# Fused cross-attention and mixture-of-experts kernel: a third buffer for weight quarters, 128-row reads of the K and Q stacks, filler products in the first slot, and a product between the two score groups

## The chip, the cores and the metric

One Trainium2 chip, one core of it. The time is device microseconds (us) from launch to end of one execution; the profiled execution also has a span, from its first to its last instruction.

## The reference

Two residual blocks over eight batches of 256 x 512. The first is a cross-attention whose positions are the 512 columns, with 16 heads of 16 channels. The second is a mixture of 12 experts, of which each of the 2048 rows uses two.

```python
q = Wq @ layernorm(x) + bq ; k = Wk @ ctx + bk ; v = Wv @ ctx + bv     # per batch, 256x512
scores = einsum('bhkt,bhks->bhts', q, k) * SCALE                       # 16 heads, 512 x 512
out = einsum('bhts,bhks->bhkt', softmax(scores), v)
x = x + tanh(g_xattn) * (Wo @ out + bo)
t = layernorm(x)                                                       # 2048 tokens of 512
probs = softmax(t @ gate_w.T); top_w, top_i = top_k(probs, 2)          # renormalised
for e in range(12):
    h = silu(t @ w1[e].T) * (t @ w3[e].T)                              # 320 wide
    y = y + h @ w2[e].T * cw[:, e:e + 1]
x = x + tanh(g_ffn) * y
```

## The kernel before

**Stages.** Each engine runs its own program, in order; semaphores join them. Attention runs first, then a short routing stage, then 43 expert tiles. Attention is a software pipeline over ten slots (`slots`, L355): slot t projects batch t ("a"), computes scores, exponentials and values of batch t-1 ("b_"), finishes batch t-2 ("c"), and prepares the input of batch t+1 ("p"). Slot 0 only projects batch 0; slots 2 to 6 do all four things; slot 7 has no "p", slot 8 has only "b_" and "c", slot 9 only "c".

**A slot.** It has 16 steps v. In a step TensorE (PE) issues the scores of step v+1 in two groups (L1190, one group for each of the PSUM tensors S0 and S1), then at most one extra product of the table `EXTRA` (steps 0 to 3: k0, k1, q0, q1; 4, 5, 6, 10: v0 to v3; 7 to 9: the output projection o0, o1; 12, 13: transposes t0, t1; 14: the gate's logits), then the values of step v (L1229). ScalarE (ACT) makes two exponentials a step (L716), 128x1024 each. VectorE (DVE) takes every product out of PSUM: k and q by L901, with a cast to a high part (L908), v by L913, the values' sums by L964 after every fourth step, o by L930, the transposes by L933. It also normalises x (L847, cast L852), casts the next context (L832, step 11), and multiplies by the inverse sums (L888, cast L890, step 5). GpSimd (POOL) subtracts each high part from its float32 source to make the low part (L575, L596).

**Quarters.** The experts' float32 weights are split into a high and a low float16 part during attention, in 48 quarters of 512 KB. ACT loads a quarter into one of two buffers `wf` (L691), DVE splits it (L812, L814; `split_quarter`) into one of two buffers `wp`, and ACT stores it (L697; `store_quarter`) and then issues the load of the quarter two later. `quarters` (L334) places the splits at steps: 2, 4, 7, 11, 12, 13 in a steady slot, 4, 7, 11, 13 in slot 1, eight in slot 8. The store of a split at step v stands in ACT's program behind the second exponential of step min(v+2, 15), so ACT waits there until the split is done.

**K and Q.** Their high and low parts are written to DRAM (L491, three parts of 256 KB each) and read back as stacks of 48 rows at partitions 0 and 64 (L498: two DMAs of 384 KB each for K and for Q), because a score product contracts 3 parts x 16 channels. SyncE (SP) issues these. In a slot its queue holds, in order: next context and x (L432, L436), the row of sums (L465, tile `zl`), eight moves of sums (L474) with the write of their inverses between them (L470), eight reads of the inverses (L481), K and Q writes, then, after all six writes have landed, all four reads, then the output (L505) and the normed tokens (L510). DVE makes the inverses (L972) at step 1, ahead of k1's copy.

Of the kernel before, what the change touches and what calls it, by code (L numbers as in the profile page):

```python
# [14 lines left out]
P = 128  # L15
# [34 lines left out]
class Signals:  # L50


    def __init__(self, sem):
# [13 lines left out]
        self.qkst = sem("qkst")  # L67
# [17 lines left out]
        self.raw = sem("raw")  # L85
        self.top = sem("top")
        self.turned = sem("turned")
        self.shift = sem("shift")
        self.shst = sem("shst")
        self.shld = sem("shld")  # L90


def flamingo_kernel(nc, x, ctx_in, g_xattn, g_ffn, WqT, bq, WkT, bk, WvT, bv, WoT, bo, gateT, wall, out):
# [28 lines left out]
    EB = 4  # L122
    HB = 2 * (FT - 1) + 1
# [5 lines left out]
    q_dram = nc.dram_tensor("q_parts", [P // DK, PARTS, DK, CT * T], F16).ap()  # L129
    k_dram = nc.dram_tensor("k_parts", [P // DK, PARTS, DK, CT * T], F16).ap()  # L130
# [10 lines left out]
    with top:  # L141
# [25 lines left out]
        wf = [sb(f"wf{i}", [P, WQ], F32) for i in range(2)]  # L167
# [17 lines left out]
        ctx_sb = [sb(f"ctx{i}", [P, CT, T], F32, att) for i in range(2)]  # L185
# [101 lines left out]
        fast = Signals(lambda name: sem("f_" + name))  # L287
        slow = Signals(lambda name: sem("g_" + name))
# [3 lines left out]
        s_rows = sem("s_rows")  # L292
# [36 lines left out]
        KQ_WRITES, KQ_READS = 16 * 2 * PARTS, 16 * 4  # L329
# [4 lines left out]
        def quarters(t):  # L334

            if t.i is None and t.add in (0, B + 1):
                return []
            if t.i is None and t.add == 1:
                steps, parts = (4, 7, 11, 13), [(At(None, 0, 0), c) for c in range(4)]
            elif t.i is None and t.add == B:  # L340
                steps = (0, 2, 4, 6, 8, 10, 12, 13)
                parts = [(At(None, 0, e), c) for e in (NE - 2, NE - 1) for c in range(4)]
            else:
                steps = (2, 4, 7, 11, 12, 13)
                if t.i is None:
                    e = [At(None, 0, 3 * ((t.add - 2) // 2) + n) for n in (1, 2, 3)]
                else:
                    e = [At(t.i, 3, n) for n in (1, 2, 3)]
                if t.add % 2 == 0:
                    parts = [(e[0], c) for c in range(4)] + [(e[1], c) for c in range(2)]  # L350
                else:
                    parts = [(e[1], c) for c in range(2, 4)] + [(e[2], c) for c in range(4)]
            return [(v, e, c) for v, (e, c) in zip(steps, parts)]
# [21 lines left out]
        s_wf = [sem(f"s_wf{i}") for i in range(2)]  # L375
# [49 lines left out]
        def _(sp):  # L425
            def attention(sp, g, guard):
# [4 lines left out]
                def load_ctx(b, par):  # L431
                    sp.dma_start(ctx_sb[par][:, :, :],  # L432
                                 c_v[bass.ds(b.value(), 1)].rearrange("b p m t -> p (b m) t")).then_inc(g.cc, 16)
# [5 lines left out]
                def slot(sp, t, par, a, b_, c, p):  # L439
# [12 lines left out]
                    if p:  # L452
# [4 lines left out]
                        wait(sp, g.cl, nxt, 1, -1)  # L457
                        load_ctx(nxt, 1 - par)
                        load_x(nxt)
                    if c:  # L460
# [5 lines left out]
                        for half in range(2):  # L466
                            for j in range(GH):
                                if (half, j) == (1, 0):
# [8 lines left out]
                        for half in range(2):  # L477
                            for j in range(GH):
# [3 lines left out]
                    if a:  # L482

                        wait(sp, g.qk, t, KQ_READS, 0, s_bog)
                        for stack, parts, dram, hi, lo, order in ((K, ks, k_dram, g.kh, g.kl, (0, 0, 1)),
                                                                  (Q, qs, q_dram, g.qh, g.ql, (0, 1, 0))):
                            wait(sp, hi, t, 1, 1)
                            for r in sorted(range(PARTS), key=lambda r: order[r]):
                                if order[r] == 1:
                                    wait(sp, lo, t, 1, 1)  # L490
                                sp.dma_start(dram[:, r], parts[:, order[r]].rearrange("p m t -> p (m t)"))\  # L491
                                    .then_inc(g.qkst, 16)

                        wait(sp, g.qkst, t, KQ_WRITES, KQ_WRITES, s_bog)
                        wait(sp, g.full, t, 2 * VS, -2 * VS)
                        for stack, dram in ((K, k_dram), (Q, q_dram)):
                            for s in range(2):
                                sp.dma_start(stack[par][64 * s:64 * s + PARTS * DK, :, :]  # L498
                                             .rearrange("p (g m) t -> p g (m t)", m=CT),
                                             dram.rearrange("(g s) r c n -> s (r c) g n", s=2)[s]).then_inc(g.qk, 16)  # L500
# [11 lines left out]
                if guard:  # L512
                    sp.wait_ge(s_rows, 4)
                load_ctx(At(None, 0, 0), 0)
# [31 lines left out]
        def _(pool):  # L546
# [9 lines left out]
            pool.wait_ge(s_pool_c, 5)  # L556
            def constants():

                pool.tensor_copy(ident16[:, :], ident[:, :]).then_inc(s_vone, 1)
# [11 lines left out]
            def attention(pool, g, guard):  # L571
# [11 lines left out]
                def slot(pool, t, par, a, b_, c, p):  # L583
                    nxt, bc = t.before(-1), t.before(2)
                    if a:
# [11 lines left out]
                    if p:  # L597
                        lo_part(nxt, cs, ctx_sb[1 - par], g.ch, g.cl)

                first = At(None, 0, 0)  # L600
# [850 lines left out]
```

## Time and profile before

| | |
|---|---|
| median of 3 runs | 824.47 us (821.6 to 824.72) |
| profiled execution, its own time | 824.88 us |
| its span | 823.1 us |
| PE busy | 646.0 us (78%) |
| DVE busy | 415.7 us (50%) |
| ACT busy | 316.8 us (38%) |
| POOL busy | 243.8 us (30%) |
| mean granted PE clock | 0.888 |

A share of busy time is a mean over stages. Attention fills the span to about 517 us; the expert tiles run from about 551 us on with PE busy throughout. "Granted clock" is TensorE's clock as the throttle let it through: 1.00 is 2.4 GHz, 0.50 is 1.2 GHz.

### The profile page before, as it was taken

Reading aid. Unit: us, or ns where it says so; the run is one execution under the profiler, and the core shown is the slowest. Engines: PE = TensorE matmul, PEld = TensorE weight load, DVE = VectorE, ACT = ScalarE, POOL = GpSimd, SP = SyncE. Lnnn points to the kernel's source line nnn. Section 1 sums busy time; section 2 is a strip of 40 time slices with the busy share of each in tenths; the row PEclk is TensorE's granted clock in tenths of the full one; section 3 lists DMA queues with packets and bytes.
Section 4 is the critical chain, followed back from the end, with each engine's and each line's share of the span. In section 5 each row is a group of like instructions: output and inputs, shape, how many; then the busy total and the mean of one; then the engine's idle time right before and its main releaser. Section 6 shows DMA issues by size and latency. Waiting matters only on the chain.

```text
span 823.1 us, 13989 instructions
## 1 busy us (share of the span) xinstructions
PE 646.0 (78%) x4217; PEld 282.8 (34%) x4218; DVE 415.7 (50%) x757; ACT 316.8 (38%) x391; POOL 243.8 (30%) x186
## 2 busy tenths in 40 slices
PE   4478897887885977978878654259999999999993
PEld 1112122212221222221221121236666666666661
DVE  5526476566584683774654843563333333333330
ACT  0047655554663554654646510002222222222221
POOL 5223123132240340331210202043344443354422
PEclk9999999889897997997987955559999999999997
DMA  6548669569579587695797636543677787754432
GB/s 205 129 104 204 209 212 293 146 191 310 156 217 293 146 227 262 192 251 159 238 251 211 203 106 230 174 156 63 174 188 195 213 242 201 204 105 92 85 51 39
DMA packets 66405, 150.82 MB, mean 183 GB/s; under 512 B 9973, under 2 KB 15606, under 8 KB 64822
## 3 DMA queue, kind: packets, MB, share of 16 engines
q1 hardware_dynamic: 34576, 72.37, 31.5%
q10 hardware_dynamic: 22150, 55.35, 20.3%
q0 software_dynamic: 9632, 22.55, 14.1%
q8 instruction: 21, 0.34, 0.2%
q14 instruction: 26, 0.21, 0.1%
HBM read 87.85 MB, written 57.93 MB: 177 GB/s over the span
## 4 chain that ended last, share of the span: by engine, by line
PE 50%; DVE 16%; DMA 15%; issue 7%; ACTq 3%; ACT 2%; SPq 2%; POOL 2%; PEldq 1%; POOLq 0%; DVEq 0%
PE S L1365 15%; PE O L1386 8%; DMA wf<-wall 8%; PE O L1229 7%; PE MA L1264 7%; DVE wp L814 4%; PE S L1190 4%; DVE wp L812 4%; DMA out<-yo,slot_out 3%; ACT prob L716 2%; PE S L1352 2%; PE MA L1246 2%; PE MC L1264 2%; ACTq L697 1%; ACTq L691 1%
## 5 line engine op out<-in xcount | busy, mean ns | idle before, releaser
L716 ACT ACTIVATE prob<-S 128x1024 f32<-128x1024 f32 x256 | 244.9, 1025 | 223.5 <-PE S L1190 121.3
L1229 PE MATMUL O<-prob,V 128*32 128x512 f32 x1024 | 154.5, 680 | 0.0
L1365 PE MATMUL S<-W,xT 128*128 x1032 | 150.1, 303 | 1.2 <-issue 1.2
L1190 PE MATMUL S<-Q,K 48*128 48x512 f16 x512 | 93.8, 421 | 69.3 <-ACT prob L716 60.1
L1365 PEld LDWEIGHTS S<-W,xT 128*128 128x128 f16 x1032 | 100.4, 99 | 38.9 <-issue 1.4
L648 POOL DMA_INDIRECT out<-yo,slot_out x43 | 68.2, 1587 | 118.3 <-ACT yo L761 65.4
L1190 PEld LDWEIGHTS S<-Q,K 48*128 48x128 f16 x512 | 19.7, 95 | 209.5 <-ACT prob L716 176.5
L1386 PE MATMUL O<-W,hT 128*128 (+1 forms) x344 | 90.3, 381 | 0.9 <-DVE hT L1161 0.9
L1149 DVE SCALAR_TENSOR_TENSOR hh<-S,act 128x320 f32<-128x320 f32 x43 | 21.1, 492 | 126.9 <-PE S L1365 126.9
L814 DVE SCALAR_TENSOR_TENSOR wp<-wf,wp 128x1024 f16<-128x1024 f32 x48 | 71.4, 1488 | 1.7
L812 DVE TENSOR_SCALAR wp<-wf 128x1024 f16<-128x1024 f32 x48 | 47.0, 979 | 41.9 <-DMA wf<-wall 41.9
L575 POOL TENSOR_TENSOR ks<-kf,ks 128x1024 f16<-128x1024 f32 x8 | 17.0, 2131 | 151.6 <-DVE ks L908 151.6
L624 POOL DMA_INDIRECT xg<-tokens_normed,slot_tok x43 | 42.4, 987 | 46.8 <-PE S L1352 34.6
L761 ACT ACTIVATE yo<-O,slot_w 128x512 f32<-128x512 f32 x43 | 29.5, 687 | 60.5 <-PE O L1386 56.3
L755 ACT ACTIVATE hs<-hh 128x320 f16<-128x320 f32 x43 | 20.2, 470 | 77.8 <-DVE hh L1149 77.8
L748 ACT ACTIVATE act<-S 128x320 f32<-128x320 f32 x43 | 18.8, 437 | 79.9 <-PE S L1365 70.3
L1386 PEld LDWEIGHTS O<-W,hT 128*128 128x128 f16 (+1 forms) x344 | 31.6, 97 | 49.3 <-issue 29.0
L575 POOL TENSOR_TENSOR os<-kf,os 128x1024 f16<-128x1024 f32 x8 | 17.4, 2178 | 89.7 <-DVE os L890 89.7
L1246 PE MATMUL MA<-w4s,cs 128*128 128x256 f16 x192 | 30.1, 300 | 16.0 <-DVE V L913 11.6
L1161 DVE COPY hT<-S 128x640 f16<-128x640 f16 x43 | 21.1, 492 | 41.0 <-PE S L1376 39.1
L1264 PE MATMUL MA<-cs,w4s 128*128 128x512 f16 x96 | 34.8, 519 | 6.9 <-DVE w4s L781 4.1
L901 DVE TENSOR_SCALAR kf<-MA,cols 128x512 f32<-128x512 f32 x16 | 12.0, 751 | 54.3 <-PE MA L1264 54.3
(145 smaller groups left out, 651.5 us busy)
## 6 DMA issues: line engine op xcount, KB each, us to landing
wf<-wall ACTq DMA_DIRECT2D x48, 512.0 KB, 7.6
weight_parts<-wp ACTq DMA_DIRECT2D x48, 512.0 KB, 6.1
W<-weight_parts SPq DMA_DIRECT2D x10, 2048.0 KB, 10.0
k_parts<-ks SPq DMA_DIRECT2D x24, 256.0 KB
q_parts<-qs SPq DMA_DIRECT2D x24, 256.0 KB
K<-k_parts SPq DMA_DIRECT2D x16, 384.0 KB, 7.3
Q<-q_parts SPq DMA_DIRECT2D x16, 384.0 KB, 10.6
ctx<-ctx_in SPq DMA_DIRECT2D x8, 512.0 KB, 10.0
```

Of the source, the lines that this page charges most:

```text
L575: pool.tensor_tensor(parts[:, 1], f[:, :, :], parts[:, 0], ALU.subtract).then_inc(lo, 1)
L624: pool.indirect_dma_start(out=xg[j % TR][:, :], out_offset=None, in_=xn_dram[:, :], in_offset=bass.IndirectOffsetOnAxis(ap=slot_tok[:, j:j ...
L648: pool.indirect_dma_start(out=out[:, :], out_offset=bass.IndirectOffsetOnAxis(ap=slot_out[:, j:j + 1], axis=0), in_=yo[j % TR][:, :], in_o ...
L716: act.activation(prob[:, u % RING, :], S[u % 2][:, :], ACT.Exp, scale=SCALE).then_inc(g.exp, 1)
L812: dve.tensor_scalar(wp[c % 2][:, 0], wf[c % 2][:, :], WS, None, ALU.mult).then_inc(s_whi, 1)
L814: dve.scalar_tensor_tensor(out=wp[c % 2][:, 1], in0=wf[c % 2][:, :], scalar=WS, in1=wp[c % 2][:, 0], op0=ALU.mult, op1=ALU.subtract).then_ ...
L1190: last = pe.matmul(S[u % 2][:, s * T:(s + 1) * T], K[par][r0:r0 + rows_, 2 * g4 + n, st * P:(st + 1) * P], Q[par][r0:r0 + rows_, 2 * g4 + ...
L1229: last = pe.matmul(O[g4 % 2][2 * DK * j:2 * DK * (j + 1), :], V[par][:, st, head(g4, j), :], prob[:, u % RING, (j % 2) * T:(j % 2 + 1) * T ...
L1246: last = pe.matmul(MA[:, i * C:(i + 1) * C], cs[:, xp, k, m * P:(m + 1) * P], w4s[:, wp_, 2, k, :], start=(n == 0 and k == 0), stop=(n == ...
L1264: last = pe.matmul(bank[:, :], w4s[:, wp_, w, k, m * P:(m + 1) * P], src[:, xp, k, :], start=(n == 0), stop=(n == 3 * CT - 1))
L1365: last = pe.matmul(ps, xT[par][:, xp * TT + k, :], W[:, bass.ds(off + (w * WCOL + (2 * k + n) * F), F)], start=(k == 0 and (xp, w) == (0, 0)),
L1386: last = pe.matmul(y_ps[:, :], hT[par][0:rows_, block, :], W[0:rows_, bass.ds(off + (w * WCOL + W2 + k * T), T)], start=(n == 0), stop=(n ...
```

## The change

- Three buffers `wf` in place of two (`WFS = 3`); a store is followed by the load of the quarter three later. The room comes from the context: one buffer in place of two, and the next context's load waits for the low part of the present one.
- The splits of a steady slot are at steps 0, 2, 5, 8, 10, 13; slot 1 has 4, 7, 10, 13; slot 8 is as before.
- The DRAM copies of K and Q get a fourth part, written once at the start (for K with 64, for Q with 0), so that a stack is read as one DMA of 128 rows (1 MB).
- SP issues K's writes, Q's two high writes, then K's read when K's writes have landed, then Q's low write, then Q's read when Q's writes have landed. The semaphore of the writes is split in two.
- The order of the moves of sums and of the reads of inverses is changed; their number is not.
- Slot 0: the low parts of the context, x, K and Q are made by DVE; POOL fills its constants in that time; PE runs filler products (128x128 float32 into an unused part of PSUM): 8 before and 8 after the first product, and the number in `BUSY` behind each projection.
- In a step PE issues the first score group, the extra product, the second score group, the values.

```diff
-            return [(v, e, c) for v, (e, c) in zip(steps, parts)]
+                steps = (0, 2, 5, 8, 10, 13)
+                first = At(t.i, 12, 4 + 6 * (t.add - 2)) if t.i is not None else At(None, 0, 4 + 6 * (t.add - 2))
+            return [(v, first.before(-n)) for n, v in enumerate(steps)]
...
-        wf = [sb(f"wf{i}", [P, WQ], F32) for i in range(2)]
+        wf = [sb(f"wf{i}", [P, WQ], F32) for i in range(WFS)]
...
-        ctx_sb = [sb(f"ctx{i}", [P, CT, T], F32, att) for i in range(2)]
+        ctx_sb = sb("ctx", [P, CT, T], F32, att)
...
-                        wait(sp, g.cl, nxt, 1, -1)
-                        load_ctx(nxt, 1 - par)
+                        wait(sp, g.cl, nxt, 1)
+                        load_ctx(nxt)
...
+                        def read(stack, dram):
+                            sp.dma_start(stack[par][:, :, :].rearrange("p (g m) t -> p g (m t)", m=CT),
+                                         dram.rearrange("(g s) r c n -> (s r c) g n", s=2)).then_inc(g.qk, 16)
...
+                        wait(sp, g.kh, t, 1, 1)
+                        write(k_dram, ks, 0, (0, 1), g.kst)
+                        wait(sp, g.kl, t, 1, 1)
+                        write(k_dram, ks, 1, (2,), g.kst)
+                        wait(sp, g.qh, t, 1, 1, s_bog)
+                        write(q_dram, qs, 0, (0, 2), g.qst)
...
+                        wait(sp, g.kst, t, KQ_WRITES, KQ_WRITES, s_bog)
...
+                        read(K, k_dram)
+                        wait(sp, g.ql, t, 1, 1, s_bog)
+                        write(q_dram, qs, 1, (1,), g.qst)
+                        wait(sp, g.qst, t, KQ_WRITES, KQ_WRITES, s_bog)
+                        read(Q, q_dram)
...
+            act.wait_ge(s_padset, 2)
+            for n, dram in enumerate((k_dram, q_dram)):
+                act.dma_start(dram[:, PARTS], wp[n][:, 0, :]).then_inc(s_pads, 16)
...
+                if q.i is not None or q.add + WFS < QUARTERS:
+                    load_quarter(q.before(-WFS))
...
+                low(first, cs, ctx_sb, g.ch, g.cl)
...
+            def keep_busy(n):
+
+                for _ in range(n):
+                    pe.matmul(O[1][:, 0:P], ones[:, :], ones[:, :], start=True, stop=True)
...
-                            scores(bb, 1 - par, v + 1)
+                            scores(bb, 1 - par, v + 1, (0,))
                         what = EXTRA.get(v, "")
                         if a and what in A_USES:
                             project(t, par, what)
+                            if not (b_ or guard):
+                                keep_busy(BUSY[what])
                         if c and what[0:2] in C_USES:
                             output(bc, what)
+                        if b_ and v + 1 < VS:
+                            scores(bb, 1 - par, v + 1, (1,))
```

## Rows read from the trace of the kernel before

**Rows 1.** The page: the chain that ended last, by line.

```profile
PE S L1365 15%; PE O L1386 8%; DMA wf<-wall 8%; PE O L1229 7%; PE MA L1264 7%; DVE wp L814 4%; PE S L1190 4%; DVE wp L812 4%; DMA out<-yo,slot_out 3%; ACT prob L716 2%; PE S L1352 2%; PE MA L1246 2%; PE MC L1264 2%; ACTq L697 1%; ACTq L691 1%
```

**Rows 2.** The chain in order of time: start us, us, what.

```profile
35.19 10.73 DMA Q<-q_parts
49.22 2.67 PE MA L1264 x6
92.78 2.64 PE MA L1264 x6
...
307.87 8.32 DMA wf<-wall
...
377.67 2.67 PE MA L1264 x6
429.61 6.92 DMA zl<-osum
480.75 3.62 PE O L1229 x16
```

**Rows 3.** Timeline of PE, one steady slot: start us, us, line, tiles, count [idle before].

```profile
266.47 2.74 PE L1264 MATMUL MA<-cs,w4s 128*128 128x512 f16 x6
271.21 1.47 PE L1264 MATMUL MA<-cs,w4s 128*128 128x512 f16 x6
272.61 1.06 PE L1229 MATMUL O<-prob,V 128*32 128x512 f32 x8
...
280.02 0.83 PE L1246 MATMUL MA<-w4s,cs 128*128 128x256 f16 x6
...
307.67 1.00 PE L1280 MATMUL MC<-ident,xn 128*128 128x128 f32 x4 [3.09 <-DVE xT L933]
...
314.79 1.06 PE L1229 MATMUL O<-prob,V 128*32 128x512 f32 x8
320.98 0.61 PE L1190 MATMUL S<-Q,K 48*128 48x512 f16 x2 [5.12 <-ACT prob L716]
```

**Rows 4.** Timelines of DVE and POOL in the same slot; last row: slot 9.

```profile
270.61 0.55 DVE L972 RECIPROCAL zr<-zl 128x64 f32<-128x64 f32 x1 [0.61 <-DMA zl<-osum]
292.57 1.23 DVE L814 SCALAR_TENSOR_TENSOR wp<-wf,wp 128x1024 f16<-128x1024 f32 x1
301.85 2.02 DVE L812 TENSOR_SCALAR wp<-wf 128x1024 f16<-128x1024 f32 x1
303.91 3.03 DVE L814 SCALAR_TENSOR_TENSOR wp<-wf,wp 128x1024 f16<-128x1024 f32 x1
300.81 2.52 POOL L596 TENSOR_TENSOR xs<-xn,xs 128x1024 f16<-128x1024 f32 x1 [2.06 <-DVE xs L956]
...
487.60 0.55 DVE L972 RECIPROCAL zr<-zl 128x64 f32<-128x64 f32 x1 [1.73 <-DMA zl<-osum]
```

**Rows 5.** SP's issues in the same slot; last row: all reads of L498.

```profile
278.16 3.22 SPq L491 DMA_DIRECT2D k_parts<-ks  x3
281.43 5.36 SPq L491 DMA_DIRECT2D q_parts<-qs  x3
298.11 0.81 SPq L498 DMA_DIRECT2D K<-k_parts  x2
...
DMA to landing us min/median/max: 5.1/8.9/13.4
```

**Rows 6.** Stretches: us, busy us (instructions) of PE, PEld, DVE, ACT, POOL, clock, DMA share, GB/s.

```profile
42.00:46.00 4.00, 0.03 (x2) 0.03 (x4) 1.06 (x1) 0.00 (x0) 2.63 (x2) 1.00 1.04 187
270.00:326.00 56.00, 44.04 (x284) 13.01 (x276) 36.61 (x53) 30.66 (x32) 15.43 (x10) 0.91 0.77 226
310.00:318.00 8.00, 5.85 (x44) 2.48 (x40) 1.70 (x3) 2.44 (x3) 0.00 (x0) 0.92 1.05 407
```

**Rows 7.** Waits: engine, line, waited for: us in total, times, longest.

```profile
PE S L1190 <- ACT prob L716: 60.1, 58, 6.8
```

**Rows 8.** Timeline of PE in slot 0.

```profile
15.50 2.72 PE L1264 MATMUL MA<-cs,w4s 128*128 128x512 f16 x6 [2.79 <-DVE kf L901]
```

More of the change, by code:

```diff
@@ L338, in quarters, with over @@
             if t.i is None and t.add == 1:
[L339 removed]
+                steps, first = (4, 7, 10, 13), At(None, 0, 0)
             elif t.i is None and t.add == B:
[L341 to L353 removed]
+                steps, first = (0, 2, 4, 6, 8, 10, 12, 13), At(None, 0, QUARTERS - 8)
+            else:
+                steps = (0, 2, 5, 8, 10, 13)
+                first = At(t.i, 12, 4 + 6 * (t.add - 2)) if t.i is not None else At(None, 0, 4 + 6 * (t.add - 2))
+            return [(v, first.before(-n)) for n, v in enumerate(steps)]
+        def over(q, d):
+            return At(q.i, q.mul // d, q.add // d)
         def slots(eng, slot):
@@ L374, in flamingo_kernel @@
         s_wr = sem("s_wr")
-        s_wf = [sem(f"s_wf{i}") for i in range(2)]
+        s_wf = [sem(f"s_wf{i}") for i in range(WFS)]
         s_whi, s_wlo = sem("s_whi"), sem("s_wlo")
@@ L476, in slot @@
                         wait(sp, g.zst, bc, 16, 16)
-                        for half in range(2):
-                            for j in range(GH):
+                        for j in range(GH):
+                            for half in range(2):
                                 dst0 = 64 * half + DK * j
@@ L482, in slot @@
                     if a:
-                        wait(sp, g.qk, t, KQ_READS, 0, s_bog)
[L485 to L492, printed above, removed]
@@ L494, in slot, with write @@
-                        wait(sp, g.qkst, t, KQ_WRITES, KQ_WRITES, s_bog)
-                        wait(sp, g.full, t, 2 * VS, -2 * VS)
[L496 to L500, printed above, removed]
+                        def write(dram, parts, part, rows_, st):
+                            for r in rows_:
+                                sp.dma_start(dram[:, r], parts[:, part].rearrange("p m t -> p (m t)")).then_inc(st, 16)
@@ L584, in slot @@
                     nxt, bc = t.before(-1), t.before(2)
-                    if a:
+                    if t.i is None and t.add == 0:
+                        if not guard:
+                            constants()
+                    elif a:
                         lo_part(t, ks, kf, g.kh, g.kl)
@@ L1002, in attention @@
                     split_projections((1,))
-                x_normed(At(None, 0, 0))
+                x_normed(first)
+                low(first, xs, xn, g.xh, g.xl)
                 slots(dve, slot)
```

139 lines of the change are left out of this document (71 added, 68 removed).

## The prediction

> **What bounds the kernel now.** I read the chain that ended last first. The transfer `wf<-wall` holds 8% of the span and the two split operations behind it 8% more [rows 1], so loading and splitting weight quarters is on the path, although DVE is busy only half of the time. The chain in order of time says where: 8.32 us in slot 5 [rows 2], the pattern of slots 2 to 6, where five such pieces stand near the slot's end. It goes like this: the split of step 11 ends, ACT stores it and only then issues the load of the quarter that DVE splits at step 13; DVE waits for it; ACT waits behind the store of that split; PE waits for the exponential. That is the 5.12 us of idle PE before the next slot's scores, and the next k0 takes 2.74 us where k1 takes 1.47 [rows 3], because the clock has dropped to its lower level in the wait. In all PE waited 60.1 us for exponentials [rows 7].
>
> The second hold-up is at t1: PE is idle 3.09 us for DVE's copy of t0 [rows 3]. DVE was in the split of step 11, whose operations took 2.02 and 3.03 us while POOL ran two subtractions; alone the second takes 1.23 [rows 4]. Each blocked operation ends 0.5 or 1.1 us after POOL's: DVE is held until POOL is done.
>
> No engine is full in a steady slot: of 56 us PE is busy 44.0, DVE 36.6, ACT 30.7, the DMA share is 0.77 [rows 6]. At the upper clock, from start to start, a step has 0.54 us of scores and 1.00 of values, a k or q product takes 1.40 and a v product 0.78; 16 steps and 13.8 us of extra products are 38.4 us [rows 3]. ACT's is 30.7 us, and about 1.3 us for each of six store-and-load pairs. What I ask is which chain is next at, say, 45 us a slot.
>
> **The change, part by part.** Time is counted from the end of a slot's last values.
>
> *Third buffer and new steps.* Each load now has five or six steps between its issue and its use, some 15 us, against the 8.32 us wait at its worst place. The wait for `wf` goes in all slots. A store now leaves three steps, some 9 us, before the second next split needs its `wp`; I cost that at nothing, and at 2 us a slot if stores land as late as Q's slow reads.
>
> *What is late next.* The slot's last sums are now copied at once, and k0 follows at once. But `zl` still needs its transfer: 6.92 us in the chain [rows 2]. DVE takes the inverses ahead of k1's copy, so k1's copy comes at about 0.7 + 6.9 + 1.0 + 0.8 = 9.4 us, and q0, which could start at 7.3, waits 2.1. Before, this wait was hidden in the stall (DVE then waited 0.61 us for `zl` [rows 4]). From the inverses to the multiplication of step 5 there are SP's writes and eight reads: 270.61 [rows 4] to 278.16, where SP starts on K [rows 5], 7.5 us, and 2.3 us for the last to land. So the multiplication is at 7.7 + 9.8 = 17.5, and it and its cast end at 19.5. From there DVE is serial (durations of the same timeline): V copies 3 x 0.35; sums of squares and means 2 x 1.55; o0, o1 and t0 copies 2.0; two copies of sums 1.2; x and the tokens normed and cast 2 x 1.7; the context cast 0.6; a wait for POOL's inverse spread 1.1; three splits of 1.9. That is 18.2 us. Three splits (steps 5, 8, 10) now each stand right behind a cast that starts a POOL subtraction, and so lose what the second operation lost in rows 4, 3.03 - 1.23 = 1.8 us: 5.4. Thus t1 can start at 43.1. From t1 to the end of the last values it took 315.85 - 307.67 = 8.2 us [rows 3], at the lower clock for most of it, and I keep that, as PE waits some 4 us before t1. A steady slot: 51.3, and I take 52 for the waits that ACT's stores still make, against (377.67 - 92.78) / 5 = 57.0 [rows 2]. Bounds: if `zl` lands in 2.4 us (in slot 9 DVE waited only 1.73 us for it [rows 4]) everything after is 4.5 earlier; if each blocked split costs the full 2.6 us of a POOL subtraction, 2.4 later.
>
> The Trainium skill (SBUF - State Buffer, section "Who interferes with whom") says that issue order decides which of the two engines is blocked when a DVE operation with two SBUF inputs meets a POOL one. By that rule the three splits lose nothing where DVE is first, and a slot would be 5.4 us shorter; the trace has the second split operation as the loser.
>
> *128-row reads.* While only K and Q reads and queued loads were left, the DMAs were full at a share of 1.04 and moved 187 GB/s; full-height transfers at the same share moved 407 [rows 6]. So 1.5 MB in half-height form cost about 8 us of all engines, and 2 MB at full height 5. In slot 0 the Q read is on the path: 10.73 us [rows 2]; 1 MB at 407 GB/s is 2.6, and with about 2 us to land 4.6 to 5: 5.5 us gained there. In steady slots reads are off the path: issued at 298.11 they had until the last step. In the new order Q's low write waits for K's writes, and Q's read for it: K's writes from 17, landing by 25; Q's low write by 32; the read landing by 39, needed at 50. Cover 11 us.
>
> *Single context buffer.* The load waits for the low part, made at about 44 us, inside the slot before; SP has nothing else to do before the next `zl`. Nothing; if it fell past the slot's end, `zl` stands behind it in SP's queue and each us is a us.
>
> *Product between the score groups.* The second group waited for an exponential 0.2 to 0.8 us in a few steps; this is the rest of the 60.1 us [rows 7] beside slot-end waits, some 2 us a slot. I take no gain, as DVE sets the slot's pace. A loss would come where the product waits (q0, t1): the second group stands behind it; the two following operations of PE, 1.3 us, cover one exponential. Nothing to -2 us a slot.
>
> *Slot 0.* DVE makes four low parts at 1.2 us where POOL took 2.1 to 2.5 [rows 4], 1 us less on the path twice; its own first operations are no longer held by POOL (about 1.8 us once); the low part of x delays k0's copy by 1.2. k1 took 2.72 us after 2.79 us of idle [rows 8], 1.47 is its time at the upper clock. Fillers should raise that, but ten behind k1 are 2.1 us or more, in front of q0, and eight ahead of the first product delay it by up to 1 us. I take 1.5 us for all this, so slot 0 gives 7; bounds 3 and 11. The pads are two DMAs among ACT's early ones, 1 us ahead of nothing.
>
> The Trainium skill (TensorE: Matmul & The Clock Gate, section "What's actually happening") says the low clock is the default and activity releases it. By it all four projections of slot 0 run in 1.4 us and slot 0 would give 4 us more than I take; by that rule the trace agrees that k1 after its wait ran at the low level, 2.72 us.
>
> *Slots 1, 7, 8.* Slot 1 took 92.78 - 49.22 = 43.6 us [rows 2]; PE's work is 33.3 and ACT's, with four pairs, 34.5: I take 35.5, a gain of 8. Slot 7 has no x, no context and one blocked split less, 5.9 us off DVE's chain, so t1 waits no more: 47. Slot 8's `zl` chain (19.5) and ten steps of 2.5 to 2.7 us, paced by ACT's eight pairs, give 46. The two took 480.75 + 3.62 - 377.67 = 106.7 [rows 2]: a gain of 13.7.
>
> Sum: 7 + 8 + 5 x 5.0 + 13.7 = 53.7 us. Slot 9, routing and expert tiles have no edit in them. The profiled execution took 824.88, the median of runs is 0.4 less, so 824.5 - 53.7 = 771.
>
> **The rivals.** *A, the slots come down to PE's and ACT's work.* If `zl` is quick or DVE wins the port, slots 2 to 6 take about 45 us: 35 us more, 736; half of it 753. For: DMA is less bunched. Against: the share is 0.77 already, and at 45 us the same bytes are 0.95.
>
> *B, the stall moves and little is left.* The clock falls in the wait for q0 and again at t1. In rows 3 a low stretch costs about 2.8 us; with the extra waits of ACT 1 us more: slots at 55, 15 us less gain, and slot 0 and 8 give half: 795.
>
> *C, slower: K and Q come too late.* Three transfers in a row now stand where two were. The writes needed 298.11 - 286.79 = 11.3 us to land [rows 5]. With 13.4 us for each, the longest landing of a stack read [rows 5], from 20 us on, Q lands at 20 + 3 x 13.4 + 1.5 = 61.7 and a slot takes 63: six slots (2 to 7) of +6, minus some 20 of the others: 840. It makes the kernel slower from 60.4 us a slot on. Against: fewer bytes are moving then than before, and cheaper ones.
>
> *D, the edits do not act.* The wait for `wf` persists since the DMAs and not the buffers limit it: gain only in slot 0 and part of slot 1, 812; within 0.5% needs even less.
>
> **How the numbers follow.** My case 0.62, A 0.13, B 0.15, C 0.04, D 0.06. The forecast is 771 us. The range takes the bounds of `zl` (5 x 4.5 = 22 down) and of B (24 up): 747 to 797, which leaves out the far ends of A and B, C and D. A measurement of this kernel tells about 0.5%, 4 us, from no change. Faster by over 0.5%: 0.92 (mine, A, B and a third of D); within: 0.03; slower: 0.05.
>
> **What would show it.** Right: no `wf` in the chain between 60 and 480 us; slots of 50 to 54 us from k0 to k0; q0 waiting 1 to 4 us for k1's copy at the start of a slot; t1 still waiting for t0's copy; the second split operation of steps 8 and 10 at about 3 us; the Q read of slot 0 landing in 4 to 6 us and slot 1's first scores near 39 us. Wrong: slots near 45 (then DVE was not the next bound), PE waiting for `Q<-q_parts` in a steady slot (C), or a clock below 0.85 over attention (B).

## The result, and the profile after

The changed kernel takes 820.56 us, the median of 20 runs (814.03 to 828.12), against 824.60 for the kernel before (816.60 to 833.82, 20 runs): a ratio of 0.9948, 95% interval 0.9922 to 0.9973. The forecast was 771, range 747 to 797. So it is faster, by 4 us where 54 were forecast, and outside the range. The profiled execution took 816.6 us, 4 us under its median; its span of 814.9 is 8.2 us less than before, and the stages below add up to these 8.2. The mean clock is 0.88.

The page's chain of the changed kernel, by line, answers to [rows 1]. `wf<-wall` is gone, as forecast; the reads of the inverse sums and SP's issues ahead of them (L470, L477) have come in, 12% together.

```profile
PE S L1393 15%; PE O L1414 9%; PE O L1253 7%; DMA ocz<-inverse_sums 5%; PE S L1214 5%; SPq L470 4%; DMA out<-yo,slot_out 3%; SPq L477 3%; DVE wp L825 3%; PE MC L1288 3%; PE MA L1288 2%; PE S L1380 2%; ACT prob L724 2%; PE MC L1308 2%; DVE wp L823 2%
```

The chain in order of time, changed kernel, for the start of k0 and what stands out ([rows 2]):

```profile
39.71 5.67 DMA Q<-q_parts
47.77 2.67 PE MA L1288 x6
...
257.28 1.56 PE MA L1288 x6
...
269.41 5.48 DMA ocz<-inverse_sums
274.92 1.24 DVE kf L904
```

From the PE timelines of both kernels, k0 of slot 1 starts at 49.16 before and 47.70 after, of slot 2 at 92.71 and 90.13, of slot 7 at 377.60 and 371.30; slot 8's values end near 484.3 and 473.9. So:

| stretch | before, us | after, us | gain | forecast gain |
|---|---|---|---|---|
| slot 0, to k0 of slot 1 | 49.2 | 47.7 | 1.5 | 7 |
| slot 1 | 43.6 | 42.4 | 1.1 | 8 |
| slots 2 to 6 | 284.9 (57.0 each) | 281.2 (56.2 each) | 3.7 | 25 |
| slots 7 and 8 | 106.7 | 102.5 | 4.2 | 13.7 |
| the rest | | | -2.3 | 0 |

Waits of the changed kernel ([rows 7] for the first):

```profile
PE S L1214 <- ACT prob L724: 46.0, 29, 4.4
ACT prob L724 <- issue: 43.5, 11, 5.1
DVE kf L904 <- DMA ocz<-inverse_sums: 32.0, 7, 5.8
PE MA L1270 <- DVE V L931: 20.3, 6, 4.6
```

Before, DVE waited 41.9 us in 9 pieces for the wall's quarter and 1.2 us in one piece for the inverse sums. After, it waits for no quarter, and 32.0 us in seven pieces for the inverse sums: one piece a slot, at the multiplication of step 5. DVE, POOL and ACT of the steady slot that starts at 256.7 ([rows 4]):

```profile
261.40 0.55 DVE L990 RECIPROCAL zr<-zl 128x64 f32<-128x64 f32 x1
274.92 1.23 DVE L904 TENSOR_TENSOR kf<-ocz 128x1024 f32<-128x1024 f32 x1 [4.10 <-DMA ocz<-inverse_sums]
277.12 2.50 DVE L823 TENSOR_SCALAR wp<-wf 128x1024 f16<-128x1024 f32 x1
287.01 3.04 DVE L825 SCALAR_TENSOR_TENSOR wp<-wf,wp 128x1024 f16<-128x1024 f32 x1
295.76 3.02 DVE L825 SCALAR_TENSOR_TENSOR wp<-wf,wp 128x1024 f16<-128x1024 f32 x1
299.92 0.68 DVE L951 COPY xT<-MC 128x512 f32<-128x512 f32 x1
...
286.45 2.52 POOL L580 TENSOR_TENSOR xs<-xn,xs 128x1024 f16<-128x1024 f32 x1 [2.58 <-DVE xs L868]
295.21 2.50 POOL L604 TENSOR_TENSOR xs<-xn,xs 128x1024 f16<-128x1024 f32 x1 [1.85 <-DVE xs L974]
...
299.01 0.56 ACTq L706 DMA_DIRECT2D weight_parts<-wp  x1
299.72 0.64 ACTq L699 DMA_DIRECT2D wf<-wall  x1
300.55 2.85 ACT L724 ACTIVATE prob<-S 128x1024 f32<-128x1024 f32 x3 [5.10 <-issue]
```

The splits of steps 8 and 10 are blocked as forecast. What the forecast priced at nothing is the last three rows: ACT's next exponentials stand behind the store of step 10's split, the store waits until that split ends at 298.8, and ACT makes no exponential for 5.10 us. PE in the same slot ([rows 3]):

```profile
277.26 0.83 PE L1270 MATMUL MA<-w4s,cs 128*128 128x256 f16 x6 [2.86 <-DVE V L931]
292.75 0.39 PE L1214 MATMUL S<-Q,K 48*128 48x512 f16 x2 [1.58 <-ACT prob L724]
293.67 0.39 PE L1214 MATMUL S<-Q,K 48*128 48x512 f16 x2 [0.52 <-ACT prob L724]
301.63 0.39 PE L1214 MATMUL S<-Q,K 48*128 48x512 f16 x2 [2.82 <-ACT prob L724]
301.95 1.11 PE L1304 MATMUL MC<-ident,xn 128*128 128x128 f32 x4
...
309.99 1.93 PE L1253 MATMUL O<-prob,V 128*32 128x512 f32 x8
```

t1 starts at 301.95 although t0's copy ended at 300.60: PE waited for the exponential. The values then take 1.93 us where a step at the upper clock has 1.07. SP's issues ([rows 5]) and the slot as a stretch ([rows 6]):

```profile
262.37 3.41 SPq L470 DMA_DIRECT2D ocz<-osum  x4
265.90 4.03 SPq L477 DMA_DIRECT2D ocz<-inverse_sums  x8
270.11 1.97 SPq L482 DMA_DIRECT2D k_parts<-ks  x3
```

```profile
257.00:313.00 56.00, 48.21 (x282) 14.46 (x281) 38.98 (x56) 32.23 (x33) 15.39 (x10) 0.87 0.77 242
```

### The profile page after: what moved, and what is told of

It reads as the page before. It is cut to its first block, busy times and chain, and to the rows that moved or that the text cites. A ratio compares the mean times of both kernels' runs of the same rounds, so it can differ in the third digit from the quotient of the medians.

```text
span 814.9 us, 14231 instructions
## 1 busy us (share of the span) xinstructions
PE 663.1 (81%) x4335; PEld 303.2 (37%) x4336; DVE 430.0 (53%) x761; ACT 325.1 (40%) x391; POOL 239.7 (29%) x184
## 3 DMA queue, kind: packets, MB, share of 16 engines
q1 hardware_dynamic: 36368, 76.56, 29.8%
## 4 chain that ended last, share of the span: by engine, by line
PE 49%; DVE 15%; DMA 12%; issue 9%; SPq 8%; POOL 2%; ACT 2%; ACTq 2%; DVEq 0%; POOLq 0%
PE S L1393 15%; PE O L1414 9%; PE O L1253 7%; DMA ocz<-inverse_sums 5%; PE S L1214 5%; SPq L470 4%; DMA out<-yo,slot_out 3%; SPq L477 3%; DVE wp L825 3%; PE MC L1288 3%; PE MA L1288 2%; PE S L1380 2%; ACT prob L724 2%; PE MC L1308 2%; DVE wp L823 2%
## 5 line engine op out<-in xcount | busy, mean ns | idle before, releaser
L724 ACT ACTIVATE prob<-S 128x1024 f32<-128x1024 f32 x256 | 253.2, 1025 | 207.8 <-PE S L1214 144.0
L1214 PE MATMUL S<-Q,K 48*128 48x512 f16 x512 | 107.9, 428 | 52.2 <-ACT prob L724 46.0
L1214 PEld LDWEIGHTS S<-Q,K 48*128 48x128 f16 x512 | 24.4, 94 | 216.9 <-ACT prob L724 149.7
L825 DVE SCALAR_TENSOR_TENSOR wp<-wf,wp 128x1024 f16<-128x1024 f32 x48 | 82.4, 1716 | 1.7
L823 DVE TENSOR_SCALAR wp<-wf 128x1024 f16<-128x1024 f32 x48 | 47.7, 993 | 0.1
L580 POOL TENSOR_TENSOR ks<-kf,ks 128x1024 f16<-128x1024 f32 x7 | 14.9, 2134 | 110.8 <-DVE ks L924 110.8
L1288 PE MATMUL MC<-os,w4s 128*128 128x512 f16 x96 | 32.9, 477 | 14.3 <-DVE os L906 12.1
L982 DVE COPY osum<-O 128x512 f32<-128x512 f32 x32 | 22.0, 687 | 40.5 <-PE O L1253 40.5
```

What stands on the lines that cost most here:

```text
L580: pool.tensor_tensor(parts[:, 1], f[:, :, :], parts[:, 0], ALU.subtract).then_inc(lo, 1)
L724: act.activation(prob[:, u % RING, :], S[u % 2][:, :], ACT.Exp, scale=SCALE).then_inc(g.exp, 1)
L823: dve.tensor_scalar(c[:, 0], w[:, :], WS, None, ALU.mult).then_inc(s_whi, 1)
L825: dve.scalar_tensor_tensor(out=c[:, 1], in0=w[:, :], scalar=WS, in1=c[:, 0], op0=ALU.mult, op1=ALU.subtract).then_inc(s_wlo, 1)
L1214: last = pe.matmul(S[u % 2][:, s * T:(s + 1) * T], K[par][r0:r0 + rows_, 2 * g4 + n, st * P:(st + 1) * P], Q[par][r0:r0 + rows_, 2 * g4 + ...
L1288: last = pe.matmul(bank[:, :], w4s[:, wp_, w, k, m * P:(m + 1) * P], src[:, xp, k, :], start=(n == 0), stop=(n == 3 * CT - 1))
```

## The experiments

Theory 1: the pace is set on DVE by the inverse sums and the blocked splits, and on ACT by what stands behind such a split (stores, and behind them exponentials). Theory 2: the product between the score groups eats the gain. Theory 3 came after the first four runs: the splits of steps 0 and 2 put large transfers beside the small ones of the inverse sums. Each run is compared with the kernel before on its own chip; the changed kernel itself stands at 0.9948, and a ratio of 0.01 is 8.2 us. Steady slots are from k0 of slot 2 to k0 of slot 7, over five.

**Each part alone.** The first adds only the third buffer, the single context buffer and the new steps to the kernel before; the second only the 128-row reads with their write order.

```diff
+    WFS = 3
...
-                steps = (2, 4, 7, 11, 12, 13)
+                steps = (0, 2, 5, 8, 10, 13)
```

> The kernel before with the third buffer, the single context buffer and the new steps, nothing else. Theory 1 (the slot's pace passes from the weight load to the chain inverse sums, multiplication of step 5, blocked splits, t1, and what follows t1): slots of 54 to 55 us, the wait for wf gone, total 3 to 8 us below the kernel before. Theory 2 (third buffer and steps do gain the forecast 5 us a slot, and the product between the score groups takes it back): slots of 52 us, total 20 to 35 us below.

> The kernel before with the 128-row reads, their pads and the new order of K's and Q's writes and reads, nothing else. Both theories: the end of the slots stays bound by the weight load, so little: 0 to 5 us below. If the DMAs' full share is what makes the load take 8 us, the cheaper reads shorten that wait by some 2 us a slot and the total falls by 10 us or more.

Quarters alone: 828.51 us, 1.0042 (0.9999 to 1.0086), steady slots 57.8; DVE waits 37.4 us for the inverse sums. Both theories had expected a gain here. Reads alone: 811.48 us, 0.9793 (0.9730 to 0.9855), steady slots 54.4, with the wait for the quarter still there (32.6 us); this is the expectation's second case, in which the reads cost the other transfers time. So the part that the forecast valued most gains nothing, and the part that it held to be hidden in steady slots gains 2.1%. Alone, the reads do more than the whole change.

**The two small edits undone**, on the changed kernel.

```diff
-                            scores(bb, 1 - par, v + 1, (0,))
+                            scores(bb, 1 - par, v + 1)
```

> The changed kernel with both score groups again ahead of the extra product. Theory 1: within 3 us of the changed kernel. Theory 2: 15 us or more faster than it, since each step with a product then takes 2.94 us and not 3.04, and the stretch behind t1 8.2 us and not 10.0.

```diff
-                for _ in range(n):
+                for _ in range(0):
```

> The changed kernel without any filler product. If the fillers behind k1 (to 23.6 us, where k1's result was copied by 21.7) hold up q0, slot 0 ends 1 to 2 us earlier without them; if they pay through the clock (q0 and q1 at 1.46 us, not 2.72), it ends 1 us later. Either way within 3 us of the changed kernel.

Groups together: 824.72, 0.9915 (0.9867 to 0.9963); no fillers: 819.40, 0.9900 (0.9845 to 0.9955). Neither can be told from the changed kernel. Without fillers k1, at 18.06, still takes 2.72 us and q0, at 21.66, takes 1.45 as with them, and k0 of slot 1 starts 1.1 us earlier, at 46.64. Theory 2 has no support in the kernel's time. The steady slots of this one execution are 55.1 us with the groups together, 1.1 less, and a step with a projection takes 3.04 us with the product between the groups and 2.94 with the groups together; so a price of about 1 us a slot may be there, where the forecast took none.

**The steps**, all on the changed kernel with its reads.

```diff
-                steps = (0, 2, 5, 8, 10, 13)
+                steps = (2, 4, 7, 11, 12, 13)
```

> The changed kernel with two buffers and the steps of before (2, 4, 7, 11, 12, 13; slot 1: 4, 7, 11, 13). Theory 3, formed after the first four runs (the splits of steps 0 and 2 put four transfers of 512 KB beside the small transfers of the inverse sums, so the multiplication of step 5 waits for them, 32 us in seven slots where it was 1.2; the third buffer and the new steps only exchange one wait for another): the wait for the inverse sums falls under 8 us, the wait for wf comes back at some 25 to 33 us, and the total is that of the reads alone, 5 to 10 us below the changed kernel. Theory 1 (blocked splits and what follows t1 set the pace): within 3 us of the changed kernel.

> The changed kernel with its three buffers but the steps of before. Theory 3: neither of the two waits is left whole: the inverse sums are on time and the load for step 13 is issued at step 9, so only the wait for the store behind wp remains, 2 to 5 us a slot; total 8 to 20 us below the changed kernel. Theory 1: no more than 3 us below it.

> The changed kernel with the splits at 0, 2, 4, 7, 9, 13: as early as in the changed kernel, but none right behind a cast that starts a subtraction on POOL, apart from the one at 4. Theory 1: t1's wait shrinks by 3 to 4 us a slot and the total falls by 15 us or more. Theory 3: the inverse sums come late as before the edit (some 30 us in all); what the splits gain shows behind step 5, 0 to 8 us.

> The changed kernel with the splits at 3, 5, 7, 9, 11, 13, so that no store or load is issued between step 0 and step 5; three of the six (3, 5, 11) stand behind a cast that starts a subtraction on POOL, as many as in the changed kernel. Theory 3: the wait for the inverse sums falls under 8 us and the total by 10 to 25 us. Theory 1: within 3 us of the changed kernel.

| quarters | buffers | us | ratio (95%) | steady slot | DVE waits for inverse sums |
|---|---|---|---|---|---|
| 2, 4, 7, 11, 12, 13 | 2 | 813.58 | 0.9832 (0.9782 to 0.9881) | 55.2 | 1.4 |
| 2, 4, 7, 11, 12, 13 | 3 | 801.60 | 0.9668 (0.9607 to 0.9728) | 53.1 | 4.4 |
| 0, 2, 4, 7, 9, 13 | 3 | 787.17 | 0.9554 (0.9506 to 0.9602) | 49.9 | 13.0 |
| 3, 5, 7, 9, 11, 13 | 3 | 809.56 | 0.9807 (0.9751 to 0.9864) | 55.9 | 3.7 |

The third buffer is worth 1.6% at the old steps, although DVE there waits 26.8 us for the stores behind `wp`, a cost that the forecast put at nothing for the new steps; the new steps then cost more than that gain. Moving three splits off the steps 5, 8 and 10, which start a POOL subtraction, makes a slot of 49.9 us, below the 52 that was forecast. The split of step 7 is one that nobody blocks (second operation 1.23 us), but the multiplication of step 5 is still late (timelines of DVE and PE, quarters at 0, 2, 4, 7, 9, 13):

```profile
270.56 1.23 DVE L825 SCALAR_TENSOR_TENSOR wp<-wf,wp 128x1024 f16<-128x1024 f32 x1
...
261.51 1.46 PE L1270 MATMUL MA<-w4s,cs 128*128 128x256 f16 x6 [4.10 <-DVE V L931]
```

The reads of the inverse sums (64 KB each) landed in 2.3 us (median) before and 2.4 with the old steps, and in 4.0 with the changed kernel's and 4.2 with 0, 2, 4, 7, 9, 13, both of which store and load two quarters in the slot's first five steps. With no split before step 3 the median is 2.4 again. That is what Theory 3 said, but at 0.9807 and 55.9 us a slot this run (with splits at 5 and 11) shows that it was not the only cause.

**Each suspected cost taken away by itself**, on the changed kernel with its own steps.

```diff
...
-                        pool.tensor_tensor(xs2[:, 1], xn2[:, :, :], xs2[:, 0], ALU.subtract)
+                        pool.tensor_tensor(xs2[:, 1, :, 0:8], xn2[:, :, 0:8], xs2[:, 0, :, 0:8], ALU.subtract)
```

> The changed kernel with GpSimd's subtractions of the low parts of the normalised activations (steps 8 and 10) cut to the first 8 columns of each half, so that they take almost nothing; the quarter steps stay at 0, 2, 5, 8, 10, 13. The low part of the second one is cleared once at the start, so both low parts are left out of the result. Theory 1 (the blocked splits of steps 8 and 10, and the store and exponentials behind them, are most of what the changed kernel pays): those two second operations fall from 3.03 us to 1.23, the exponentials of step 10 no longer stand behind the store, a steady slot is 3 to 5 us shorter, 785 to 800 us in all. Theory 3 (most is the wait for the inverse sums at step 5, which this doesn't touch): that wait stays at 32 us, a steady slot at 54 to 56 us, 808 to 818 us in all.

799.31 us, 0.9736 (0.9679 to 0.9793), steady slots 53.6. The second split operation falls from 1716 to 1263 ns in the mean. One part of the expectation failed: ACT still waits behind the store of step 10's split, though that split is no longer blocked. The grouped row, and ACT in one slot:

```profile
L828 DVE SCALAR_TENSOR_TENSOR wp<-wf,wp 128x1024 f16<-128x1024 f32 x48 | 60.6, 1263 | 1.7
...
290.32 3.77 ACT L727 ACTIVATE prob<-S 128x1024 f32<-128x1024 f32 x4 [3.44 <-issue]
```

```diff
-                        wait(sp, g.zst, bc, 16, 16)
-                        for j in range(GH):
-                            ...
-                                sp.dma_start(zc[dst0:dst0 + DK, :, :], src).then_inc(g.oz, 16)
```

> The changed kernel without SyncE's eight reads of the inverse sums per slot; the attention output is then multiplied by itself and a constant in place of the inverse sums, so the normalisation is left out (one operation of the same 128x1024 size on VectorE). It prices the whole way of the inverse sums. Theory 3: VectorE no longer waits at step 5 (32 us in seven slots before), TensorE's 2.9 us at the third value product go, and a steady slot is 3 to 5 us shorter; 785 to 800 us. Theory 1 with the blocked splits as the main price: the time won at step 5 is given back at steps 8 to 11, a slot is under 1.5 us shorter; 808 to 820 us. The tail may differ by some us, since the routing follows from other values.

790.83 us, 0.9592 (0.9531 to 0.9654), steady slots 52.2. The first form of the expectation held, 29 us in all: DVE's wait is gone, and PE's 2.9 us for V's copy too. The waits for exponentials remain (PE, 53.0 us in 41 pieces).

```diff
-                            if u == 2 * min(v + 2, VS - 1) + 1:
+                            if u == 2 * min(v + 3, VS - 1) + 1:
```

> The changed kernel with every quarter's store issued one step later by ScalarE (three steps behind its split in place of two), nothing else moved. If the exponentials of steps 10 and 11 wait because the store in ScalarE's order stands behind a blocked split, the waits of TensorE for the exponentials fall (46.0 us in 29 pieces in the changed kernel) and a steady slot is 1 to 2 us shorter: 806 to 815 us. If the store is not what holds ScalarE, or if the later stores then hold up the splits two steps on through the two buffers of split weights: 820 to 830 us, with a new wait of VectorE for those buffers.

800.96 us, 0.9720 (0.9654 to 0.9786): 19 us less than the changed kernel for one step's delay in ACT's order, more than expected. Its waits, against 46.0 and 32.0 above:

```profile
DVE kf L904 <- DMA ocz<-inverse_sums: 26.4, 7, 5.8
PE S L1214 <- ACT prob L724: 14.3, 24, 2.5
```

> Both single edits together: GpSimd's low parts of the normalised activations cut to 8 columns of each half (the same values left out as in the run with the short low parts, 0.974), and every store one step later (0.972 alone). If both hit one cause, the exponentials that stand behind the store of a blocked split, the two together give no more than one alone: 0.968 to 0.975, some 797 to 803 us. If the length of the blocked split on VectorE costs something of its own (as the forecast's sum had it, 5.4 us a slot), together they give 0.950 to 0.960, 782 to 790 us.

780.63 us, 0.9491 (0.9447 to 0.9535), steady slots 50.2. Alone the two edits win 2.1% and 2.3%, together 4.6%, so they remove two different costs. One is the longer split on DVE's own chain. The other is the place of the stores in ACT's program, and the block of steps 8 and 10 is not what makes it cost: the later stores win as much with the splits of steps 8 and 10 unblocked (0.9736 to 0.9491) as with them blocked. In steady slots the later stores, added to the short subtractions, take away only 2 us of PE's idle time (29.8 to 27.7) but 15 us of its busy time (238.2 to 223.5), with the granted clock going from 0.86 to 0.92. The edit moves all stores but that of step 13, which stands at step 15 either way, and which of them matters was not isolated. In this run PE waits for a Q read at slot 8's start, 2.9 us (the read is in the chain at 376.20 with 9.82 us, behind K's and Q's writes with 11.02 and 10.12): this is the order of transfers of the forecast's rival C. The run with 0, 2, 4, 7, 9, 13 has slots of 49.9 us without such a wait.

**Toward a better version**, same edit to the steps.

> The changed kernel with its quarters at steps 0, 4, 7, 9, 12, 13 in place of 0, 2, 5, 8, 10, 13: only one split left beside the inverse sums, and none at a step that starts a GpSimd subtraction (as in the run with 0, 2, 4, 7, 9, 13, whose slots took 49.9 us and still waited 13.0 us in seven slots for the inverse sums). Theory 1 and 3 together: the wait for the inverse sums is under 5 us in all, the slots 48 to 50 us, 775 to 787 us in all. Rival: steps 12 and 13 stand close together and wait for the low part of the context or for the store of step 9 (26.8 us of that wait in the run with the old steps), slots 51 us or more, 790 to 805 us.

784.33 us, 0.9510 (0.9445 to 0.9575), steady slots 50.9 (one of the six executions took 3305.72 us, the others 776.97 to 787.93; the ratio leaves it out, and nothing here explains it); the wait for the inverse sums is 4.2 us in all. But the neighbours 12 and 13 put two stores and two loads just ahead of the read of the sums (`zl`), and in one slot that read landed some 9 us after its issue at 290.18 (ACT, DVE and PE timelines):

```profile
284.13 0.56 ACTq L706 DMA_DIRECT2D weight_parts<-wp  x1
284.84 0.62 ACTq L699 DMA_DIRECT2D wf<-wall  x1
287.15 0.56 ACTq L706 DMA_DIRECT2D weight_parts<-wp  x1
287.86 0.63 ACTq L699 DMA_DIRECT2D wf<-wall  x1
...
300.00 0.55 DVE L990 RECIPROCAL zr<-zl 128x64 f32<-128x64 f32 x1 [5.75 <-DMA zl<-osum]
...
301.61 2.74 PE L1288 MATMUL MA<-xs,w4s 128*128 128x512 f16 x6 [5.33 <-DVE kf L917]
```

> The version with the quarters at steps 0, 4, 7, 9, 12, 13 (0.951) with two quarter buffers in place of three: a load is issued two splits ahead, so the splits of steps 9 and 13 have one 6 us stretch between load and use. If the third buffer is needed there, VectorE waits for the wall's quarter 15 us or more in all and the ratio is 0.960 or above. If the steps alone do it, the ratio stays at 0.951 within 0.006 and that wait is under 8 us.

> The changed kernel with its quarters at steps 0, 4, 7, 9, 11, 13: as the version with 12 and 13 (0.951), but no two splits at neighbouring steps, so no two stores and loads stand together ahead of the read of the sums at a slot's start (one of its slots waited 5.75 us for that read and TensorE 5.33 us). If the small reads behind neighbouring quarters are what is left: 0.943 to 0.949, and no wait for the read of the sums over 3 us. If the split of step 11, which meets the subtraction of the context's low part, costs as much through its store: 0.950 to 0.960.

> The version with the quarters at steps 0, 4, 7, 9, 12, 13 (0.951) with both score groups ahead of the extra product, as in the kernel before. On the changed kernel this made no difference that could be told (0.991 against 0.995). If TensorE's other waits hid a cost of the product between the groups, it shows here: 0.939 to 0.946. If not: 0.948 to 0.954; and if the product between the groups helps, 0.956 or above.

Two buffers at these steps: 782.26, 0.9509 (0.9461 to 0.9558), a wait for the quarter of 6.6 us in all. So at these steps the third buffer is worth nothing that can be told. Groups together: 784.69, 0.9526 (0.9480 to 0.9572), again no difference. Split 12 moved to 11: 800.81, 0.9721 (0.9667 to 0.9774), a miss. Step 11 casts the context and starts POOL's subtraction, so this split is blocked, and ACT and PE stand behind it:

```profile
288.82 2.03 DVE L823 TENSOR_SCALAR wp<-wf 128x1024 f16<-128x1024 f32 x1
290.89 3.02 DVE L825 SCALAR_TENSOR_TENSOR wp<-wf,wp 128x1024 f16<-128x1024 f32 x1
...
295.56 1.94 ACT L724 ACTIVATE prob<-S 128x1024 f32<-128x1024 f32 x2 [4.80 <-issue]
...
294.64 1.11 PE L1304 MATMUL MC<-ident,xn 128*128 128x128 f32 x4 [3.95 <-DVE xT L951]
```

One split moved by one step costs 2.1%, about 3 us a steady slot. The versions that compute all and beat both kernels are those with the quarters at 0, 4, 7, 9, 12, 13 (0.951, with two buffers as well) and 0, 2, 4, 7, 9, 13 (0.955).

## Why the prediction was wrong

The sum wanted 53.7 us, the span gave 8.2. Of the missing 45.5, 21.3 are in slots 2 to 6, 9.5 in slots 7 and 8, 6.9 in slot 1, 5.5 in slot 0. The last 2.3 come after them, in stages that were not edited; some 1.6 of these lie between slot 9's multiplication and the landing of the first tile's rows, and no run tests why.

- **The third buffer.** "The wait for `wf` goes in all slots": it did. That a gain follows was not shown: alone, at the new steps, the wait for the inverse sums came in its place, and the kernel was no faster. At the old steps it did gain, 1.6%.
- **From the inverses to the multiplication, 9.8 us.** Mis-sized: it takes 13.5 (261.40 to 274.92). SP's second four moves and eight reads are issued slower (3.41 and 4.03 us for these groups, 2.51 and 3.76 before), and the last read lands in 5.48 us where I took 2.3. I took these durations from a slot whose first split was at step 2 and moved a split to step 0 without asking what its store and load do to the small transfers. It was masked in the slot's total since `zl` landed 3 us sooner than the 6.92 I took, so q0 never waited, and the multiplication came at +18.2 where I had +17.5. The experiment without these reads prices the whole way at 29 us, 4.1 in a steady slot.
- **DVE's serial chain.** Right in its length: 23.6 us forecast from the end of the cast to t0's copy, 23.7 measured (276.87 to 300.60). The blocked splits of steps 8 and 10 took 3.04 and 3.02 us as forecast, and step 5's lost on its first operation, 2.50 against 0.68.
- **ACT beside it: the step that failed most.** I costed DVE's splits on DVE alone, and named only t0's copy as what t1 waits for. ACT stands behind each split's store, which its program has two steps later, and PE behind ACT: 5.10 us of ACT, and for PE 1.3 us more before t1 and 1.58 and 0.52 earlier in the slot, behind the split of step 8. Of the 5.10 us the block made some 1.7 by my estimate, as 3.44 remained in a slot without it; the rest comes from DVE reaching that split late. Then "from t1 to the end 8.2 us, and I keep that" became 10.0: the last step's values ran at the lower clock (1.93 us, 1.06 before), and the second score group now stands behind t1 (0.54). Putting the stores one step later gives back 19 us, cutting the subtractions 17, both 38. The forecast slot was 51.3 (52 taken); this one took 55.1, their mean is 56.2.
- **The clock.** The sum priced the lower clock only behind t1. That k0 follows at once did pay: k0 and k1 of the five steady slots took 14.9 us of PE in place of 20.9. But behind the waits for V's copy and for exponentials the other products slowed: the values took 97.9 us in place of 94.8 (687 ns each in place of 668), the v products, the output projection, the transposes and the gate's logits 57.0 in place of 51.8, so the 6.0 us were lost again. These are sums of one execution of each kernel, and whether faster products would only have met the next wait is not shown.
- **128-row reads, "off the path in steady slots".** Wrong: alone they take 2.6 us off a steady slot and 2.1% off the whole. I looked at whether PE waits for K and Q, and not at what else the half-height transfers delay. In that run the wait for the quarter falls from 41.9 to 32.6 us, and the median landing of the quarters' stores from 6.1 to 5.0 us and of their loads from 7.6 to 7.1; which of these makes the gain was not isolated.
- **Slot 0, 7 us.** The Q read fell from 10.73 to 5.67 us, as forecast. But it is issued at 39.71, not 35.19: Q's low write, issued at 30.95 right behind K's 1 MB read, lands in 8.75 us (4.48 before). With the reads alone that write goes at 28.21, lands in 8.47, and slot 1's first scores start at 42.40, against 45.43 with the whole change and the 39 of the forecast. The low parts on DVE and the fillers were to give 1.5 us together, and slot 0 lost by them: k0's copy starts at 17.40 (14.69 before) and K's first write is issued at 22.47 (20.01 before, 19.35 with the reads alone, 22.32 in the changed kernel without fillers). The fillers bought nothing that can be told: without them slot 0 was 1.1 us shorter.
- **Slot 1 and slot 7.** I took sums of work, "PE's work is 33.3 and ACT's, with four pairs, 34.5: I take 35.5" (the terms given, 30.7 and four times 1.3, make 35.9). Slot 1 took 42.4, though DVE was idle half of it. Its pace is set step by step by whichever engine is slower there. With a projection PE is busy throughout, 3.04 us (k1 at 53.10, q0 at 56.14); with a v product too, 2.40 (62.23 to 64.63), and ACT waits 0.29 for the next scores; without a product ACT runs on without a gap, 1.95 a step (four steps from 81.03 to 88.81):

```profile
62.33 2.11 ACT L724 ACTIVATE prob<-S 128x1024 f32<-128x1024 f32 x2 [0.29 <-PE S L1214]
64.73 2.11 ACT L724 ACTIVATE prob<-S 128x1024 f32<-128x1024 f32 x2 [0.29 <-PE S L1214]
...
81.84 5.68 ACT L724 ACTIVATE prob<-S 128x1024 f32<-128x1024 f32 x6
```

  By these rows 4 x 3.04 + 4 x 2.40 + 8 x 1.95 = 37.4 us is my estimate of the slot without stalls: an engine's sum of work falls short of a slot where the slower engine changes from step to step. The other 5 us are k0 and the first values at the lower clock (2.74 and 1.94 us) and PE's waits for exponentials; with the stores one step later slot 1 took 38.8. Slots 7 and 8 repeat the waits of the steady ones: in slot 7 PE waits 3.29 us for V's copy behind the late multiplication and 3.91 for an exponential ahead of t1.
- **The Trainium skill** (SBUF - State Buffer, "Who interferes with whom": the first to issue keeps the port, the other blocks) agrees with the rows. POOL's subtractions start at 286.45 and 295.21, the second split operations at 287.01 and 295.76, and DVE is the one that loses each time. In the run with 0, 2, 4, 7, 9, 13 it is the other way round once: DVE's second split operation starts at 276.38 and keeps its 1.23 us, and POOL's small operation for the inverse spread, at 276.50, takes 1.67 us where it took 0.71 elsewhere. The gain of 5.4 us a slot needed DVE to be first with its second operation; right behind the cast that releases POOL it was not, in any row shown here.
- **The clock in slot 0.** k0 took 1.70 us, k1 2.72 (the lower level) after 7.11 us of idle behind four fillers, q0 and q1 1.46. Without any filler k0 and k1 took 2.72, q0 and q1 1.45, so only k0 gained by them; before, all four took 2.72. The Trainium skill (TensorE: Matmul & The Clock Gate, "What's actually happening") says that the low clock is the default and that activity releases it; k1 behind its idle time agrees, and the 4 us more that the prediction worked out beside it did not come, as slot 0 gave 1.5 in all.

Of the rivals, B (the stall moves, 795) came nearest, with its extra waits of ACT and its lower clock at t1, at too small a price: it counted 1 us a slot for ACT and no late inverse sums. The wait for q0 that it names did not come, and the clock over the steady slots stayed at 0.88, above the 0.85 that was its sign. The stated range is 2 us wider on either side than its own terms (771 less 22 is 749, and 24 more is 795), which changes nothing.

## What to carry to other kernels

When a split, copy or any instruction is moved, price it on every queue that waits for its end, not only on its own engine: here the store in ScalarE's order carried VectorE's lateness to the exponentials and to TensorE, and one step's distance was worth 19 us. Give such work the steps in which no other engine's subtraction has just been released, and keep large transfers away from the moment at which a short chain of small ones sets the next product. A wait that goes away proves nothing about the next one: take the next chain's durations from a place with the traffic that the change will bring. And look at TensorE's busy time beside its idle time: when the later stores were added to the short subtractions, 15 of the 17 us won in the steady slots came from faster products and only 2 from shorter waits.

## What the runs showed of the hardware that was not expected

- The 64 KB reads of the inverse sums land in 2.3 to 2.6 us (median) in the kernel before and in the runs with the steps of before, and in 4.0 to 4.9 in all runs with splits at steps 0 and 2, whose 512 KB stores and loads go through another queue at that time. One read of the sums (`zl`) landed some 9 us after its issue behind four such transfers. The Trainium skill (DMA: Bandwidth & Descriptors, "Queues, rings and completion order") says that a DMA engine takes turns between queues a packet at a time, which would make a small transfer wait for its neighbour's packets; the rows agree in direction, none shows the packets themselves.
- The issue of a load by ScalarE took 0.5 us mostly, and 2.48 us in one slot of the run with late stores, while SyncE's two issues of Q's writes (at 261.47 too) took 4.87 us (2.37 in the slot of the changed kernel above); the next exponentials start behind it. The run with 0, 2, 4, 7, 9, 13 has it as well, 2.21 us at 257.52 beside 4.34 from 256.91.

```profile
261.47 2.48 ACTq L699 DMA_DIRECT2D wf<-wall  x1
264.13 2.86 ACT L724 ACTIVATE prob<-S 128x1024 f32<-128x1024 f32 x3 [2.62 <-PE O L1253]
```
